# Score buffers of the attention stream: three banks for the first pass, three one-bank units for the second, eight half-size probability buffers

## What is computed

```python
x = x + _L0_attn_a_ref(_layernorm(x), ...)   # 16 heads of 8, causal, scores / sqrt(128)
x = x + _L0_ffn_ref(_layernorm(x), ...)      # sqrt((x cos(th))^2 + (x sin(ph))^2)
x = x + _L0_attn_b_ref(_layernorm(x), ...)   # 16 heads of 8, rope, not causal, scores / sqrt(8)
x = x + _L0_ffn_ref(_layernorm(x), ...)
```

## Time and profile before

| | us |
|---|---|
| median of 3 runs | 2047.44 |
| lowest, highest | 2046.84, 2049.26 |
| the profiled execution, its own time | 2051.5 |
| its span, first to last instruction | 2049.7 |
| PE, DVE busy over the span | 1692.7, 1413.4 |
| ACT, POOL busy over the span | 1060.3, 519.6 |
| exponentials (L500), 448 | 427.4 |
| maxima, rope layer (L757), 512 | 336.7 |
| maxima, causal layer (L752), 512 | 228.9 |

### The profile page before, as it was taken

The page is one execution under the profiler, slowest core; times in us unless marked ns, Lnnn a source line. Parts: engine busy times, 40 slices in busy tenths (PEclk is TensorE's granted clock), DMA queues, the critical chain, the costliest instruction groups (busy, mean ns, idle before and its releaser), DMA issues. The chain is left out here.

```text
span 2049.7 us, 36773 instructions
## 1 busy us (share of the span) xinstructions
PE 1692.7 (83%) x12704; PEld 943.6 (46%) x12781; DVE 1413.4 (69%) x4005; ACT 1060.3 (52%) x1727; POOL 519.6 (25%) x579
## 2 busy tenths in 40 slices
PE   3788888889998899887599999989997867778566
PEld 1333333333333333322366666666665645546454
DVE  6677777688777787773266666666665488655786
ACT  1466666656666666666344444434442444333453
POOL 5455555553233312300100000000001422200222
PEclk9899999999999999999799999999999977799898
DMA  5334232222222112200000000000000000000000
GB/s 95 56 61 95 62 66 51 45 45 43 48 48 34 27 36 47 47 2 1 0 2 2 2 1 2 2 3 1 2 2 1 1 0 0 1 0 0 6 16 21
DMA packets 56690, 49.82 MB, mean 24 GB/s; under 512 B 9220, under 2 KB 54468, under 8 KB 56516
## 3 DMA queue, kind: packets, MB, share of 16 engines
q1 hardware_dynamic: 53692, 46.45, 12.2%
q10 hardware_dynamic: 2824, 1.11, 0.4%
HBM read 7.10 MB, written 2.10 MB: 4 GB/s over the span
## 5 line engine op out<-in xcount | busy, mean ns | idle before, releaser
L500 ACT ACTIVATE at_probs<-ps 128x1024 f32<-128x1024 f32 (+1 forms) x448 | 427.4, 962 | 280.3 <-PE ps L613 274.2
L757 DVE TENSOR_REDUCE at_M<-ps 128x1 f32<-128x512 f32 x512 | 336.7, 686 | 111.1 <-PE ps L589 110.3
L589 PE MATMUL ps<-at_KS,at_QS 96*128 96x512 bf16 (+3 forms) x1024 | 322.4, 352 | 53.7 <-DVE at_M L752 20.9
L752 DVE CUSTOM_DVE_ANT_0 at_masked<-ps,at_mask_row 128x384 bf16<-128x384 f32 (+3 forms) x512 | 228.9, 486 | 75.7 <-PE ps L589 73.6
L630 PE MATMUL ps<-at_probs,at_V 128*9 128x512 f32 (+3 forms) x2048 | 232.8, 527 | 27.5 <-ACT at_C L508 12.3
L613 PE MATMUL ps<-at_QS,at_KS 128*128 128x512 bf16 x947 | 242.2, 342 | 14.4 <-DMA at_QS<-at_nmT 6.6
L589 PEld LDWEIGHTS ps<-at_KS,at_QS 96*128 96x128 bf16 x1024 | 91.8, 99 | 334.8 <-DVE at_M L757 150.9
L1245 DVE SCALAR_TENSOR_TENSOR la_phiq<-ps,la_ezq 128x512 f32<-128x512 f32 x64 | 44.3, 691 | 146.5 <-ACT la_ezq L1097 146.5
L380 POOL TENSOR_SCALAR_AFFINE_SELECT at_probs<-at_probs 128x256 f32<-128x256 f32 (+1 forms) x192 | 93.5, 489 | 181.1 <-ACT at_probs L500 180.1
L613 PEld LDWEIGHTS ps<-at_QS,at_KS 128*128 128x128 bf16 x1024 | 93.1, 99 | 81.5 <-issue 26.1
L839 POOL TENSOR_TENSOR la_rstd<-la_vare,mhalf 128x4 f32<-128x4 f32 x16 | 16.1, 1008 | 435.8 <-DVE la_vare L834 435.8
(11 more groups left out here) (258 smaller groups left out, 3394.9 us busy)
## 6 DMA issues: line engine op xcount, KB each, us to landing
at_QS<-at_splitq SPq DMA_DIRECT2D x288, 64.0 KB
at_KS<-at_splitk SPq DMA_DIRECT2D x279, 64.0 KB
out<-X SPq DMA_DIRECT2D x8, 256.0 KB, 2.3
at_QS<-at_nmT ACTq DMA_DIRECT2D x64, 8.0 KB
at_KS<-at_splitk ACTq DMA_DIRECT2D x9, 64.0 KB
w_raw<-fp_weights SPq DMA_DIRECT2D x1, 560.0 KB, 5.6
w_wv<-L_attn_a_wv SPq DMA_DIRECT2D x1, 512.0 KB, 6.9
w_wo<-L_attn_a_wo SPq DMA_DIRECT2D x1, 512.0 KB, 6.5
```

The source lines that it names most:

```text
L500: act.activation(v(probs[u % 4][:]), v(src), ACT.Exp, scale=layers[layer(n)]["scale"])\
L589: last = pe.matmul(ps[:, FIRST + U % 2, o * stride:o * stride + width], QS[n % 2][0:SHIFT_AT, h, qt * P:(qt + 1) * P], KS[n % 2][0:SHIFT_A ...
L752: last = v.tensor_tensor_reduce(masked[U % 4][:, o * stride:o * stride + width], src[:, o, :], mask_row[:, 512 - width:512], 1.0, 4 * NEG, ...
L757: v.tensor_reduce(M[gq % 2][:, heads[0]:heads[-1] + 1, qt], src, AX.X, ALU.max).then_inc(max_free, 1)
```

## The change

- `score_units`: the second pass has one head per unit where there were pairs (rope: 16 units a quad in place of 8; causal: 11 in place of 6, with the tile of 256 columns in two pairs, and that of 128 with four heads as before). Every second unit now fits in one bank.
- PSUM: `FIRST` has banks 0 to 2 (before 0 and 1), `SECOND` 3 to 5 (before 2 to 5). PE waits for the maxima of unit U - 3 and for the exponential of unit u - 3, where it was U - 2 and u - 2 before.
- `probs`: eight buffers of 512 columns in place of four of 1024. An exponential waits for the sum that frees unit u - 8.
- `stream_order`: new due times for the second units; all others keep theirs.

```diff
--- before.py
+++ after.py
@@ -89,12 +89,12 @@
 
     if not causal:
         first = [(qt, (j,), 512, 512) for qt in range(4) for j in range(4)]
-        second = [(kt, pair, 512, 512) for kt in range(4) for pair in ((0, 1), (2, 3))]
+        second = [(kt, (j,), 512, 512) for kt in range(4) for j in range(4)]
         return first, second
     first = [(0, (0, 1, 2, 3), 128, 128), (1, (0, 1), 256, 256), (1, (2, 3), 256, 256)]
     first += [(qt, (j,), (qt + 1) * 128, 512) for qt in (2, 3) for j in range(4)]
-    second = [(kt, pair, (4 - kt) * 128, 512) for kt in (0, 1) for pair in ((0, 1), (2, 3))]
-    second += [(2, (0, 1, 2, 3), 256, 256), (3, (0, 1, 2, 3), 128, 128)]
+    second = [(kt, (j,), (4 - kt) * 128, 512) for kt in (0, 1) for j in range(4)]
+    second += [(2, (0, 1), 256, 256), (2, (2, 3), 256, 256), (3, (0, 1, 2, 3), 128, 128)]
     return first, second
 
 
@@ -111,12 +111,12 @@
     for n in range(2 * seqs):
         if n < seqs:
             f_at = [u / 11 for u in range(11)]
-            s_at = [0.04, 0.20, 0.36, 0.50, 0.66, 0.82]
+            s_at = [0.03, 0.11, 0.19, 0.27, 0.35, 0.43, 0.50, 0.57, 0.66, 0.74, 0.83]
             sum_at = [0.50, 0.78, 1.03, 1.17]
             copy_at, tail_at = 1.19, 1.50
         else:
             f_at = [u / 16 for u in range(16)]
-            s_at = [(i + 0.20) / 8 for i in range(8)]
+            s_at = [(i + 0.20) / 16 for i in range(16)]
             sum_at = [(kt + 1.45) / 4 for kt in range(4)]
             copy_at, tail_at = 1.20, 1.44
         t0 = QUADS * (n - 1)
@@ -221,7 +221,7 @@
     M = [sb(f"M{i}", [P, 4, 4]) for i in range(2)]
     nm = sb("nm", [P, 2, 4, 4], BF16)
     nmT = [sb(f"nmT{i}", [32, P], BF16) for i in range(4)]
-    probs = [sb(f"probs{i}", [P, 1024]) for i in range(4)]
+    probs = [sb(f"probs{i}", [P, 512]) for i in range(8)]
     C = sb("C", [P, 4, P])
     rden = sb("rden", [P, 4, 4])
     O = sb("O", [P, 4, P])
@@ -244,7 +244,7 @@
     waves = sb("waves", [P, 2 * P])
 
 
-    FIRST, SECOND, SUMS, MISC = 0, 2, 6, 7
+    FIRST, SECOND, SUMS, MISC = 0, 3, 6, 7
     misc = ps[:, MISC, :]
     misc4 = misc.rearrange("p (t c) -> p t c", t=4)
 
@@ -375,7 +375,7 @@
                 return
             _, heads, width, stride = second_of(n)[i]
             u = seconds(gq) + i
-            diagonal = probs[u % 4][:].rearrange("p (h c) -> p h c", c=stride)[:, 0:len(heads), 0:P]
+            diagonal = probs[u % 8][:].rearrange("p (h c) -> p h c", c=stride)[:, 0:len(heads), 0:P]
             g.wait_ge(scores_free, u + 1)
             g.affine_select(out=diagonal, in_=diagonal, compare_op=ALU.is_ge, fill=0.0, base=0,
                             pattern=[[0, len(heads)], [1, P]], channel_multiplier=-1).then_inc(probs_masked, 1)
@@ -491,13 +491,12 @@
 
             _, heads, width, stride = second_of(n)[i]
             u = seconds(gq) + i
-            b = u % 2
-            src = ps[:, SECOND + 2 * b:SECOND + 2 * b + 2, :].rearrange("p a c -> p (a c)")
+            src = ps[:, SECOND + u % 3, :]
             v = lambda t: t.rearrange("p (h c) -> p h c", c=stride)[:, 0:len(heads), 0:width]
             act.wait_ge(scores_ready, u + 1)
-            if u >= 4:
-                act.wait_ge(sums_ready, freed_by(u - 4))
-            act.activation(v(probs[u % 4][:]), v(src), ACT.Exp, scale=layers[layer(n)]["scale"])\
+            if u >= 8:
+                act.wait_ge(sums_ready, freed_by(u - 8))
+            act.activation(v(probs[u % 8][:]), v(src), ACT.Exp, scale=layers[layer(n)]["scale"])\
                 .then_inc(scores_free, 1)
 
         def take_sums(n, q, gq, i):
@@ -582,11 +581,11 @@
             if q % 2 == 0 and u == 0:
 
                 pe.wait_ge(stack_loaded[q // 2], 16 * STACK_DMAS * (n + 1))
-            if U >= 2:
-                pe.wait_ge(max_free, U - 1)
+            if U >= 3:
+                pe.wait_ge(max_free, U - 2)
             for o, j in enumerate(heads):
                 h = 4 * q + j
-                last = pe.matmul(ps[:, FIRST + U % 2, o * stride:o * stride + width],
+                last = pe.matmul(ps[:, FIRST + U % 3, o * stride:o * stride + width],
                                  QS[n % 2][0:SHIFT_AT, h, qt * P:(qt + 1) * P], KS[n % 2][0:SHIFT_AT, h, 0:width],
                                  start=True, stop=True)
             last.then_inc(max_ready, 1)
@@ -605,12 +604,12 @@
                 pe.wait_ge(nm_loaded[q], 16 * (n + 1))
                 if gq == 0:
                     pe.wait_ge(signs_loaded, 16 * 2)
-            if u >= 2:
-                pe.wait_ge(scores_free, u - 1)
+            if u >= 3:
+                pe.wait_ge(scores_free, u - 2)
             for o, j in enumerate(heads):
                 h = 4 * q + j
-                bank, c = SECOND + 2 * (u % 2) + o * stride // 512, o * stride % 512
-                last = pe.matmul(ps[:, bank, c:c + width], KS[n % 2][:, h, kt * P:(kt + 1) * P],
+                c = o * stride
+                last = pe.matmul(ps[:, SECOND + u % 3, c:c + width], KS[n % 2][:, h, kt * P:(kt + 1) * P],
                                  QS[n % 2][:, h, 512 - width:512], start=True, stop=True)
             last.then_inc(scores_ready, 1)
 
@@ -628,7 +627,7 @@
                     continue
                 for o, j in enumerate(heads):
                     last = pe.matmul(ps[32 * j:32 * j + DH + 1, SUMS, 512 - width:512], V[n % 2][:, kt, 4 * q + j, :],
-                                     probs[(seconds(gq) + u) % 4][:, o * stride:o * stride + width],
+                                     probs[(seconds(gq) + u) % 8][:, o * stride:o * stride + width],
                                      start=kt == 0, stop=kt == 3, tile_position=(0, 32 * j))
             last.then_inc(sums_ready, 1)
 
@@ -741,7 +740,7 @@
         def maxima(n, q, gq, u):
             qt, heads, width, stride = first_of(n)[u]
             U = firsts(gq) + u
-            src = ps[:, FIRST + U % 2, :].rearrange("p (h c) -> p h c", c=stride)[:, 0:len(heads), 0:width]
+            src = ps[:, FIRST + U % 3, :].rearrange("p (h c) -> p h c", c=stride)[:, 0:len(heads), 0:width]
             v.wait_ge(max_ready, U + 1)
             if u == 0 and gq > 1:
                 v.wait_ge(nm_ready, gq - 1)
```

## The result

The changed kernel took 2036.54 us, median of 7 runs (2033.36 to 2040.46), against 2047.44 (2040.21 to 2049.69) before: ratio 0.9948, 95% interval 0.9932 to 0.9965. It is faster, by 11 us, and 37 were forecast. Its profiled execution took 2037.72 us, span 2035.9, against 2051.5 and 2049.7.

The account below looks back on a forecast made before the run. No engine is full; PE and DVE wait for each other through two first-pass banks. Rope -3.0 us an item (-24) and causal -1.6 (-13) make -37 us, from 2047.4 to 2010 us, forecast's own range 1970 to 2038, overall 1972 to 2066.

Parts of the forecast that it names:

- the third bank: First pass: PE may run three units ahead of DVE, giving back 4.3 us a rope item and 2.6 a causal item.
- PE's floor: PE's own need per key tile, eight pipelined matmuls and a sum, 2.74 us; next limit, 0.20 above DVE.
- 0.2 + 0.4 + 0.7 = 1.3: Costs in a rope item: 0.2 at the long stall, 0.4 for the smaller second-pass ring, 0.7 for later sums.
- My expected signs: Rope item: maxima's waits for PE under 12, about 10 us; long stall some 4.5; ACT busy near 48; items 61 and 48.
- +1.37 us: Second pass: extra ACT time per rope quad from one-head exponentials, 8.18 to 9.55 us; 71 us more in both layers.
- The sums: Sums at key tile ends have 0.21 us less net cover behind exponentials, costing 0.7 us a rope item, bounds 0 to 3.4.
- Rival (c): Each key tile's sum becomes the clock, losing its cover behind ACT or POOL; slower, 2081 us; chance 0.15.
- -2.6 + 1.0 = -1.6: Causal item: third bank returns 2.6 us, masks, lead and table loads cost 1.0; times 8 gives -13 us.
- 0.2 at the table loads: Causal item: cost of 0.2 us at ACT's table loads, as at the rope item's long stall.
- The term of 0.8 for masks and lead: Causal sums: 0.32 us less lead at five sums late by POOL, half taken; POOL's masks grow 3.4 us an item.
- The ring of the second pass: Four banks shrink to three; PE stops earlier during ACT's table loads: 0.4 us a rope item, bounds 0 to 0.8.
- The buffers: Eight half-size probability buffers hold what four whole ones held and wait for the same key tiles: no effect.

Follow-up runs that it names:

- e4: Changed kernel, but PE only two first-pass units ahead of DVE, as before the change, banks still rotating over three; 2070.2 us, ratio 1.0099 to the kernel before.
- e11: Changed kernel without the square root's table loads (a copy in its place) and without POOL's causal masks; 1948.3 us, causal item 44.5.
- e12: Kernel before without the square root's table loads (a copy in its place) and without POOL's causal masks; 1983.7 us, causal item 46.5.
- e5: Changed kernel with a copy in place of the square root, so no table loads for it, masks kept; 1984.8 us, causal item 47.7.
- e6: Kernel before with a copy in place of the square root, so no table loads for it, masks kept; 2002.3 us, causal item 47.1.
- e14: Changed kernel without the root's table loads, causal sums of the first three key tiles due later (0.57, 0.85, 1.06 of the quad); 1988.5 us, causal item 48.2.
- e13: Changed kernel without the root's table loads, one POOL mask for two one-head units (7 a quad, not 11); 1974.3 us, causal item 47.0.
- e1: Changed kernel with the causal layer's second and third one-head units due later (0.195 and 0.23 of the quad); 2040.0 us, ratio 0.9942 to the kernel before.
- e17: Changed kernel with one POOL mask per two one-head units and the causal second and third units due later; 2035.2 us, ratio 0.9944 to the kernel before.
- e16: Changed kernel without POOL's masks, causal second and third units due later (0.195 and 0.23 of the quad); 1996.1 us, causal item 46.9.
- e15: Changed kernel, table loads kept, with one POOL mask for two one-head units (7 a quad, not 11); 2031.5 us, ratio 0.9919 to the kernel before.

## Why the prediction was right in one layer and wrong in the other

Forecast were 37 us, measured 11. The rope layer gave nearly what was forecast. What failed is the causal layer's sum: its costs, put at 1.0 us an item, were 3.1.

**Bound, and the third bank, rope layer: right in kind, the total in part by luck.** Forecast 61.3 us an item, measured 61.6; -24 us, measured -21.2 over the eight periods. Two engines waiting for each other, one bank more, PE's floor as the next limit: a key tile without other work takes 2.83 us now (655.73 to 658.56), against the 2.74 I gave as floor. e4 shows that it is the bank. It also shows that the item's -3.0 us came out partly by luck: the bank gave back 3.2 us where I had 4.3, and all the rest cost 0.2 where I had 0.2 + 0.4 + 0.7 = 1.3. Both sizes were too big, and the errors cancel. My expected signs were too bright: 15 waits of the maxima, not under 12, and 12.7 us, not 10; 0.25 and 0.34 us ahead of four or three maxima in a row, not 0.2 or less; a long stall of 3.55 us, not 4.5. The term "+1.37 us" of ACT a quad was mis-sized: ACT was busy 43.8 us an item, not near 48, so it became +0.3 (42.5 to 43.8). Exponentials that follow each other overlap, 0.48 to 0.50 us from start to start where one takes 0.60. In both layers together they went from 427.4 to 458.6 us, 31 more and not 71: 75 ns for each of the 416 instructions, not 171.

**The sums, rope layer: half right.** They now wait for ACT in 14 places, 5.1 us more in all where I had 0.7. By e4 all three cost terms together came to 0.2 us, not 1.3, so PE must have had the time for most of these waits; what each term cost by itself wasn't measured. Rival (c) named the right row and gave it the wrong weight.

**Second pass, causal layer: the step that failed.** The sum "-2.6 + 1.0 = -1.6" an item came out at +1.1. The first term was not far off: the item is 2.0 us shorter in e11 than in e12. The costs were not 1.0 but 3.1. Against e4 the split is another, with the same sum: the bank gives 1.1 and the costs are 2.2. Of these, the term "0.2 at the table loads" rested on rows of the rope layer, where an exponential stood between table load and copy before as well. In the causal layer none did, and the new due times put two there, with the second table load: 2.4 us of delay on ACT. The list of due times was in the diff, and this could have been read from it. How much of the 3.1 this place makes isn't settled, since moving it away in e1 didn't shorten the mean item. The term of 0.8 for masks and lead was also too small (2.6 us alone, e5 with e6 against e11 with e12; 1.7 by the shortest items), and neither later sums (e14) nor fewer masks (e13) brought much of it back. I had set the masks' 3.4 us beside POOL's 23 idle us an item, and not beside the 11 us in which POOL has no idle time. What I did not ask at all is what the longer stall does to the granted clock: it fell in all five windows of the changed kernel, and in two of five before. In the rope layer an item with such a fall is 1.6 us longer; in the causal layer the price is open.

**The ring of the second pass** I priced at 0.4 us at the table loads. As the change was made it is hardly seen in the causal layer (e11, and the 0.5 us row), where the due times are spread evenly. In the rope item PE's weight loads wait for exponentials twice, 2.6 us in all; what that cost was not measured. e1 and e17 show the waits once the causal times are bunched, 4.4 us an item, but not a price: e16 has them too.

**The buffers** I put at "nothing, either way". ACT's 17.2 us of "remote" waits over five causal items speak against it; no run changed the buffers alone.

**The total.** -21.2 in the rope layer, +7.6 in the causal one, +1.5 before it and -1.7 behind the stream make the -13.8 of the spans; the medians give -10.9.

What stays open: how masks, tables and clock share the 3.1 us of the causal layer. Each alone suffices for most of it. No repair inside the causal layer that leaves no work out brought it back. The kernel before has causal items of 49.7 us with a window at 0.97 and with one at 1.00.

## What to carry to other kernels

Count buffers by what a queue in order must step over: a third bank paid here, where PE's sum of 0.98 us and a round trip of 0.42 outlast the 1.27 us of maxima in two banks, and PE has time to get ahead. A stage that is cut finer gets new places in every other queue's order, so read the list of each engine again, layer by layer, and look at what now stands between a table load and a copy that a third engine waits for. And apply such a change where it pays only: the rope layer alone gave 24 us, twice what both layers gave.

## What the runs showed of the hardware

Exponentials of 512 columns in a row cost ACT less than the row of one says. Four in a row take 2.06 us, as long as two of 1024 columns at 1.02 each, where one alone takes 0.60:

```profile
655.95 2.06 ACT L499 ACTIVATE at_probs<-ps 128x512 f32<-128x512 f32 x4 [0.81 <-PE ps L612]
```

Each of the five causal projections of k from 134 to 383 us in the changed kernel came after 3.78 us without a matmul. Four took 2.01 to 2.07 us, at the lower clock level, and one 1.66, partly at it. The same wait in e15 was once followed by 1.23 us, nearly the full level (at 201.09). In the kernel before, waits of 1.56 us were followed by the lower level in some items (2.08 us for the projection at 198.01) and by the full one in others (1.12 at 247.98).
